# Padding rows by plain transfers, 71 blocks, four output buffers and a last norm in two groups, in a two-layer attention and expert kernel

## The reference

```python
def _layernorm(x, axis=-1, eps=1e-05):
    m = jnp.mean(x, axis=axis, keepdims=True)
    v = jnp.var(x, axis=axis, keepdims=True)
    return (x - m) / jnp.sqrt(v + eps)
...
        E_FFN = 8
        E_ZERO = 4
        TOP_K = 2
        logits = jnp.einsum('btd,ed->bte', x, gate_w) + expert_bias
        topk_logits, topk_idx = jax.lax.top_k(logits, TOP_K)
        topk_w = jax.nn.softmax(topk_logits, axis=-1)
        onehot = jax.nn.one_hot(topk_idx, E_TOT, dtype=x.dtype)
        w = jnp.einsum('btk,btke->bte', topk_w, onehot)
        w_ffn = w[..., :E_FFN]
        w_zero = jnp.sum(w[..., E_FFN:], axis=-1)
        h = jax.nn.silu(jnp.einsum('btd,efd->btef', x, w1))
        y = jnp.einsum('btef,edf->bted', h, w2)
        out = jnp.einsum('bte,bted->btd', w_ffn, y) + w_zero[..., None] * x
        return out
...
    x = _layernorm(x + _L1_ffn_ref(x, L1_ffn_gate_w, L1_ffn_expert_bias, L1_ffn_w1, L1_ffn_w2), axis=-1)
```

## Time and profile before

| | us |
|---|---|
| runs: median | 1774.31 |
| runs: lowest to highest, of 3 | 1770.64 to 1775.97 |
| profiled execution | 1760.04 |
| its span on the core | 1758.3 |
| TensorE busy in the span | 1458.9 (83%) |
| VectorE, ScalarE, GpSimd busy | 930.9, 696.8, 498.6 |

### The profile page before, as it was taken

The page is one execution under the profiler, slowest core; times in us unless marked ns, Lnnn a source line. Parts: engine busy times, 40 slices in busy tenths (PEclk is TensorE's granted clock), DMA queues, the critical chain, the costliest instruction groups (busy, mean ns, idle before and its releaser), DMA issues.

```text
span 1758.3 us, 31304 instructions
## 1 busy us (share of the span) xinstructions
PE 1458.9 (83%) x10329; PEld 957.5 (54%) x10330; DVE 930.9 (53%) x3473; ACT 696.8 (40%) x959; POOL 498.6 (28%) x419
## 2 busy tenths in 40 slices
PE   3688898888889739999469999999998719999990
PEld 1245454454455416666334556555555419999990
DVE  2667768777787411111256656765753343444334
ACT  1144443544544501111036666766676402222223
POOL 4032234234233311212111123132222233444441
PEclk7788888888997859999779999999999859999995
DMA  6744335255252122533153536434526323444445
GB/s 159 196 106 96 84 95 130 80 124 113 71 97 82 50 67 72 130 87 85 36 111 82 116 78 138 111 84 107 125 64 181 136 70 63 70 71 72 72 60 200
DMA packets 118701, 174.52 MB, mean 99 GB/s; under 512 B 17159, under 2 KB 100513, under 8 KB 112432
## 3 DMA queue, kind: packets, MB, share of 16 engines
q1 hardware_dynamic: 95376, 147.65, 34.1%
q0 software_dynamic: 20928, 23.56, 8.6%
q10 hardware_dynamic: 2272, 1.70, 0.4%
HBM read 107.32 MB, written 72.82 MB: 102 GB/s over the span
## 4 chain that ended last, share of the span: by engine, by line
PE 64%; DVE 13%; issue 6%; DMA 4%; ACT 3%; POOL 2%; SPq 0%; DVEq 0%; POOLq 0%; ACTq 0%
PE ST L705 9%; PE OT L723 9%; PE ST L1797 7%; PE shared L1809 6%; PE ST L1263 6%; DVE scratch L1097 4%; PE shared L1452 3%; PE shared L749 3%; PE OT L1271 3%; PE shared L1271 3%; PE shared L766 2%; PE shared L797 2%; PE shared L814 2%; PE shared L1458 1%; PE shared L741 1%
## 5 line engine op out<-in xcount | busy, mean ns | idle before, releaser
L838 ACT ACTIVATE arena<-ST 128x1024 f32<-128x1024 f32 x416 | 414.6, 1024 | 264.0 <-PE ST L705 262.4
L1097 DVE CUSTOM_DVE_ANT_0 scratch<-shared,mask 128x512 bf16<-128x512 f32 (+3 forms) x512 | 228.8, 486 | 86.9 <-PE shared L814 71.8
L705 PE MATMUL ST<-arena 96*128 96x256 bf16 (+2 forms) x1792 | 253.1, 278 | 14.6 <-DMA arena<-qk_parts 13.7
L723 PE MATMUL OT<-arena,v_aug 128*32 128x256 f32 (+1 forms) x3584 | 252.9, 384 | 3.9 <-POOL arena L1165 1.7
L705 PEld LDWEIGHTS ST<-arena 96*128 96x128 bf16 (+1 forms) x1792 | 159.1, 102 | 114.2 <-issue 51.7
L814 PE MATMUL shared<-arena 96*128 96x512 bf16 (+3 forms) x512 | 126.7, 325 | 52.9 <-DVE mx L1097 21.7
L1910 POOL DMA_INDIRECT sum<-arena,block_to_row x72 | 113.5, 1577 | 171.2 <-DMA sum<-arena,block_to_row 128.1
L723 PEld LDWEIGHTS OT<-arena,v_aug 128*32 128x32 f32 x3584 | 85.4, 111 | 117.9 <-issue 69.9
L1165 POOL TENSOR_SCALAR_AFFINE_SELECT arena<-arena 128x512 f32<-128x512 f32 (+1 forms) x96 | 78.7, 820 | 238.4 <-ACT arena L838 238.4
L1809 PE MATMUL shared<-arena 128*128 x576 | 136.5, 380 | 0.0
L814 PEld LDWEIGHTS shared<-arena 96*128 96x128 bf16 x512 | 43.1, 103 | 132.7 <-issue 63.3
(11 more groups left out here) (208 smaller groups left out, 2338.9 us busy)
## 6 DMA issues: line engine op xcount, KB each, us to landing
arena<-qk_parts SPq DMA_DIRECT2D x224, 128.0 KB, 7.1
qk_parts<-qk_src SPq DMA_DIRECT2D x64, 384.0 KB, 2.6
arena<-qk_parts SPq DMA_DIRECT2D x32, 384.0 KB, 4.5
block_rows<-slot_x SPq DMA_DIRECT2D x72, 130.0 KB, 2.4
arena<-qk_parts SPq DMA_DIRECT2D x32, 256.0 KB, 5.3
sum<-x_out SPq DMA_DIRECT2D x16, 512.0 KB, 2.9
arena<-in_experts_inter SPq DMA_DIRECT2D x7, 1024.0 KB, 5.2
arena<-in_experts_out SPq DMA_DIRECT2D x7, 1024.0 KB, 9.5
```

The lines of the kernel that those rows point to most:

```text
L705: mm = pe.matmul(ST[n % 2][:, i * 256 + at:i * 256 + at + nq], K[par][0:rows, h, kb * P:(kb + 1) * P], Q[par][0:rows, h, q0:q0 + nq], star ...
L723: mm = pe.matmul(OT[32 * i:32 * i + 32, q0:q0 + nq], v_aug[par][:, kb, g * GH + i, :], PT[n % RING][:, i, at:at + nq], start=(u == 0), sto ...
L838: act.activation(PT[n % RING][:, :, :], ST[n % 2][:, :].rearrange("p (h n) -> p h n", h=GH), func, scale=ATT_SCALE).then_inc(L["exp"], 1)
L1097: taken = dve.tensor_tensor_reduce(out=junk[n % 2][:, at:at + m], in0=bank[:, at:at + m], in1=mask[:, 0:m], scale=1.0, scalar=LOW, op0=ALU ...
```

## The change

Four edits in one.

1. `pad_rows`: the padding rows are written by plain transfers at a row number read from `t_pad`, for four experts on SP in place of step `("sv", 2)` and for four on ScalarE ahead of the scaling of step `("xs", 2)`. Both wait for `D_PADS`. The eight scatters of `d_pool` are gone. SP's save of the last batch moves behind its first four block loads, and two waits for the saves leave SP's list.
2. `NBLK` is 71. 8192 rows at most, in eight segments, can't start more than 71 blocks of 128 (64, and 7 for the rests). The loops have `LAPS` = 17, the rest is written out.
3. `by` has four buffers, and ScalarE waits for the add of block j − 4. The wait for block j − 2 is now GpSimd's, ahead of its add.
4. The norm has two groups, of five chunks and three, instead of 3 + 3 + 2. Statistics and root are no longer mixed. Of the first five chunks GpSimd writes one row of four (`e_pool`) and ScalarE three; of the last three VectorE writes two and ScalarE two (before: ScalarE all four of six chunks, VectorE three of the last two).

```diff
-NBLK = 2 * NTOK // P + E1
+NBLK = 2 * NTOK // P + E1 - 1
+LAPS = NBLK // 4
...
+        def pad_rows(eng, experts):
+
+            eng.wait_ge(d_chain, D_PADS)
+            settle(eng)
+            for e in experts:
+                row = eng.value_load(t_pad[0:1, e:e + 1], min_val=0, max_val=ZROW)
+                eng.dma_start(slot_x1[bass.ds(row, P), :], no_row[:, :]).then_inc(d_pad, 16)
...
                     elif step == "sv":
+                        if turn.kind == "ninth" and n == 2:
+                            pad_rows(sp, range(0, E1 // 2))
+                            continue
                         save_rows(sp, L, turn, n, sum1)
             slots(sp, emit)
-            for i in range(2):
-                sp.wait_ge(L["x_saved"][i], NB // 2 * 16)
...
                     elif step == "xs":
+                        if turn.kind == "ninth" and n == 2:
+                            pad_rows(act, range(E1 // 2, E1))
                         keep_rows(act, L, turn, n, ROUTE1)
...
-        by = [carve(D) for _ in range(2)]
+        by = [carve(D) for _ in range(RX)]
...
             for j in range(RX):
                 load(j, j)
+            save_rows(sp, LC, Turn("ninth", NB + 1), 2, sum1)
...
-                if not isinstance(j, int) or j >= 2:
-                    act.wait_ge(d_added[(i + 2) % RX], lap * 16 + (16 if i >= 2 else 0))
-                act.activation(by[par], Y_BANK[par][:, 0:D], ACT.Identity, scale=b_gain[:, i:i + 1]
+                wait(act, d_added[i], lap * 16)
+                act.activation(by[i], Y_BANK[par][:, 0:D], ACT.Identity, scale=b_gain[:, i:i + 1]
...
         def d_pool(pool):
-            pool.wait_ge(d_chain, D_PADS)
-            pool.wait_ge(s_zero, 1)
-            for e in range(E1):
-                pool.indirect_dma_start(out=slot_x1,
-                                        out_offset=bass.IndirectOffsetOnAxis(ap=t_pad[:, e:e + 1], axis=0),
...
             def emit(j, i, lap):
 
+                if not isinstance(j, int) or j >= 2:
+                    pool.wait_ge(d_added[(i + 2) % RX], lap * 16 + (16 if i >= 2 else 0))
...
-        E_GROUPS = [(0, 3), (3, 6), (6, N_E)]
-        BY_DVE = {c: (3 if c >= 6 else 0) for c in range(N_E)}
+        E_GROUPS = [(0, 5), (5, N_E)]
+        BY_DVE = {c: (2 if c >= 5 else 0) for c in range(N_E)}
+        BY_POOL = {c: (1 if c < 5 else 0) for c in range(N_E)}
...
+        def e_pool(pool):
+            for g, (c0, c1) in enumerate(E_GROUPS):
+                pool.wait_ge(e_root, g + 1)
+                for c in range(c0, c1):
+                    for t in range((c + 1) * EB - BY_POOL[c], (c + 1) * EB):
+                        pool.tensor_scalar(out=e_all[:, t, :], in0=e_all[:, t, :], scalar1=e_mv[:, t, 0:1],
+                                           scalar2=e_small[:, 2, t:t + 1], op0=ALU.subtract, op1=ALU.mult
+                                           ).then_inc(e_by_pool, 1)
...
-                more = stats(*E_GROUPS[g + 1]) if g + 1 < len(E_GROUPS) else iter(())
-                together(root(c0, c1), more, 1)
+                all_of(root(c0, c1))
+                if g + 1 < len(E_GROUPS):
+                    all_of(stats(*E_GROUPS[g + 1]))
```

More of the change, by code:

```diff
@@ L1750, in d_sp, with refill @@
                 load(j, j)
-            with sp.Fori(0, NBLK // RX - 1) as it:
-                for i in range(RX):
[L1754 to L1761, removed]
+            save_rows(sp, LC, Turn("ninth", NB + 1), 2, sum1)
+            def refill(j, i):
+                sp.wait_ge(d_t, j + 1)
+                settle(sp)
+                sp.wait_ge(d_told, j * 2 + 2)
+                settle(sp)
+                load(j + RX, i)
+            with sp.Fori(0, LAPS - 1) as it:
+                for i in range(RX):
+                    refill(it * RX + i, i)
+            for j in range((LAPS - 1) * RX, NBLK - RX):
+                refill(j, j % RX)
         T_BANK = shared[0]
@@ L1826, in four @@
                     down(j, par, j - 1)
-            passes(pe, NBLK // RX - 1, four)
-            for j in range(NBLK - 3, NBLK):
+            passes(pe, LAPS - 1, four)
+            for j in range((LAPS - 1) * RX + 1, NBLK):
                 if j + 1 < NBLK:
@@ L1839, in blocks @@
                 emit(j, j, 0)
-            with eng.Fori(1, NBLK // RX - 1) as it:
+            with eng.Fori(1, LAPS) as it:
                 for i in range(RX):
                     emit(it * RX + i, i, it)
-            for j in range(NBLK - RX, NBLK):
+            for j in range(LAPS * RX, NBLK):
                 emit(j, j % RX, j // RX)
@@ L1911, in emit @@
                     out=sum1, out_offset=bass.IndirectOffsetOnAxis(ap=b_to_row[:, i:i + 1], axis=0),
-                    in_=by[i % 2], in_offset=None, bounds_check=NTOK + S - 1, compute_op=ALU.add
+                    in_=by[i], in_offset=None, bounds_check=NTOK + S - 1, compute_op=ALU.add
                     ).then_inc(d_added[i], 16)
@@ L1924, in build @@
         e_load = [sem(f"e_load{i}") for i in range(N_E)]
-        e_chain, e_root, e_by_dve, e_by_act, e_out = (
-            sem(x) for x in ("e_norm_chain", "e_root_ready", "e_rows_by_dve", "e_rows_by_act", "e_out"))
-        E_GROUPS = [(0, 3), (3, 6), (6, N_E)]
-        BY_DVE = {c: (3 if c >= 6 else 0) for c in range(N_E)}
+        e_chain, e_root, e_by_dve, e_by_act, e_by_pool, e_out = (
+            sem(x) for x in ("e_norm_chain", "e_root_ready", "e_rows_by_dve", "e_rows_by_act", "e_rows_by_pool", "e_out"))
+        E_GROUPS = [(0, 5), (5, N_E)]
+        BY_DVE = {c: (2 if c >= 5 else 0) for c in range(N_E)}
+        BY_POOL = {c: (1 if c < 5 else 0) for c in range(N_E)}
         def of_rows(ap, i):
@@ L1934, in rows_of @@
             at = c * EB + BY_DVE[c]
-            return range(c * EB, at) if by_dve else range(at, (c + 1) * EB)
+            return range(c * EB, at) if by_dve else range(at, (c + 1) * EB - BY_POOL[c])
         def e_sp(sp):
@@ L1950, in e_sp @@
                 settle(sp)
+                by_pool += BY_POOL[c]
+                wait(sp, e_by_pool, by_pool)
+                settle(sp)
                 sp.dma_start(of_rows(out, c), e_rows[c]).then_inc(e_out, 16)
             sp.wait_ge(e_out, N_E * 16)
+        def e_pool(pool):
[6 more added lines that the diff above has]
+                                           ).then_inc(e_by_pool, 1)
         def e_act(act):
@@ L2048, in _ @@
             d_pool(pool)
+            e_pool(pool)
 def shape_constants():
```

4 lines of the change are left out of this document (1 added, 3 removed).

## The result

The changed kernel takes 1758.54 us (median of 4 runs, 1752.37 to 1759.35), the kernel before 1774.56 in the same comparison (4 runs). The ratio is 0.9904, with a 95% interval of 0.9876 to 0.9931: 16.0 us gained by the medians, 17.0 by the ratio, 12 to 22 by the interval. Forecast were 18.1 us and 1756.

The account below looks back on a forecast made before the run. TensorE was taken to bound the block loop, a chain of waits the handover, load waits then VectorE and ScalarE the last norm. 10.5 + 3.7 + 0 + 3.9 = 18.1 us off the 1774.31 median gives 1756, range 1749 to 1765.

Parts of the forecast that it names:

- Padding rows: Handover into the expert blocks: with eight scatters off GpSimd's queue, it moves from 1438.61 to 1428.1, 10.5 us gained.
- (c): Handover: the padding writes stretch the token scatters to 6.4 us, total 1760; chance 0.10.
- (d): Handover gains nothing, as the save or a padding row lands as late as now: 1766.6 us; chance 0.06.
- The clock: Start of the blocks: same slow start at half clock expected, 0; one block more or fewer at half clock is ±1.8 us.
- One block fewer: Block loop: one pitch of the up product less, 3.7 us gained; 0 taken for the written-out tail.
- Four buffers: Block loop: ScalarE is freed but TensorE's loss, from VectorE's wait, stays; 0 gained, between 0 and 1.7 us.
- rival (a): Head of the block loop loses its 1.7 us after all, because adds come earlier: 1754.5 us; chance 0.08.
- Rival (e): Block loop: with the new wait the adds become the bound, slower, 34 us at a landing of 8.5: 1790; chance 0.03.
- GpSimd's row: Last norm: a row on GpSimd takes 0.6 us, bounds 0.34 to 2.6, hidden below ScalarE's 1.5 us for three rows.
- Rival (b): Last norm: GpSimd's rows over 1.5 us hold the writes; at 2.6 the norm loses 1.3 us: 1761; chance 0.11.
- Its second form: Last norm: by the port rule VectorE's root waits five GpSimd rows of 0.6, taking 3.0 us from the sum: 1759.
- Last norm: End of the kernel: ScalarE ends 3.0 us earlier and the last writes queue less, together 3.9 us gained.

Follow-up runs that it names:

- pads_alone: Kernel before with the padding edit alone: plain transfers on SP and ScalarE, last save behind the first four loads; 1747.94 us, ratio 0.9939.
- own_rows: Changed kernel with row numbers and gains of the first twelve blocks in columns of their own, those blocks written out; 1741.03 us, ratio 0.9895 to the kernel before.
- four_buffers: Kernel before with four buffers of block outputs and the moved wait alone; 1759.6 us, ratio 1.0005.
- two_rows: Changed kernel with GpSimd writing two of four rows of the norm's first five chunks, ScalarE two; 1763.03 us, ratio 0.9938 to the kernel before.
- no_pool_share: Changed kernel with no norm rows on GpSimd, ScalarE doing all four of the first five chunks; 1743.86 us, ratio 0.9922 to the kernel before.
- warm: Changed kernel with twelve more 128x512 products on TensorE between the counts and the first block; 1741.35 us, ratio 0.9908 to the kernel before.
- warm15: Changed kernel with fifteen more products on TensorE between the counts and the first block; 1755.8 us, ratio 0.9887 to the kernel before.

## Why the prediction was right or wrong

The time and the sign were right: the forecast 18.1 us lies inside both intervals (12 to 22 and 11 to 24.5 us), 1.4 to 2.1 us above the gains of the medians and 0.4 to 1.1 above those of the ratios. Term by term, from the traces:

- **Padding rows, 10.5.** Right in mechanism and size: 26.5 to 26.9 us from the counts to the first turn became 15.9 to 16.1, 10.7 on average. As named, the landing of the token scatters is late next, so rivals (c) and (d) fall. Landing of the plain transfers was bounded at 2.1 to 6.4 and taken near 2.1; it is 2.2 to 3.2 in pads_alone.
- **The clock, 0 ± 1.8.** Before, first turn to third up product is 12.02, 9.74, 9.25, 9.74 and 9.74; with the padding edit 9.81, 9.79, 11.47, 11.78, 11.88, 11.67. Two groups of values, 2 us apart, in both kernels. The prediction's ±1.8 for a block more or less at half clock is that difference. That the mean is 1.0 us higher with the edit can be chance; these profiles show neither a loss nor that there is none. What the prediction left out is that the slow start can be had back: 7.55 with TensorE kept busy.
- **One block fewer, 3.7.** Right: 3.73 in the traces, 3.5 by the ratio.
- **Four buffers, 0.** Right, and for the reason given. own_rows takes the named wait away and TensorE's loss with it; rival (a) is refuted by four_buffers. Rival (e), the adds as the bound, is refuted by 223.00 of 223.00 us busy on TensorE.
- **GpSimd's row, 0.6.** The term that was mis-sized: it was scaled by elements from the two-tensor addition, but takes 1.21. No row of before had one tensor and two scalars a partition, and the far end kept in the text, 2.6, was as near by ratio. That the miss cost nothing is in part luck: the row stays under the 1.5 us of ScalarE's three rows, with a margin of 0.3 us where 0.9 was reckoned. Rival (b) put its point of decision there; two_rows crosses it, with 2.4 us a chunk against 1.0, and loses 4.6 to 4.7 us. Its second form, the root held by the port, was priced at 3.0 us: the second root takes 2.56 us in the changed kernel and 2.43 in no_pool_share, 0.13 more.
- **Last norm, 3.9.** First load to end is 33.9 us on average in the five profiles with the old norm (33.3 to 34.4) and 29.7 in the seven with the new one as it is (29.2 to 29.9), some 4.3 less. Behind ScalarE's first row it is 3.3 us where the sum has 3.3 to 3.4; the earlier start was put at 0.6 and is 1.0 on average. As the time to that first row moves by 1 us by itself with either norm, an excess of 0.4 can't be told from the landing of the loads.
- **The sum.** From the traces it is 19.5 without the clock's column, 1.4 above the forecast, while the runs lie 0.4 to 2.1 below it; where the difference goes stays open. The prediction carried the 14.3 us between the profiled execution and the median along as a constant of the kernel. It is not: the kernel before takes 1759.2 and 1758.6 us on two chips and 1774.5 on a third, so this profile is most likely of another chip than the runs. That the absolute time came out at 1758.5 for 1756 is thus owed to the subtraction from the median of the same comparison.

## What to carry to other kernels

Here eight transfers stood behind eight others on one queue, though all sixteen only had to be finished at the same time. Moved to two queues that stood idle, they no longer counted, and the gain was the distance between the two landings, 10.5 us forecast and 10.7 found. Of two waits for the same adds in one loop, removing ScalarE's, 10.6 us long, gave nothing; the one that mattered was found from the row in which the bounding engine waits, followed one step back to the buffer that it guards. Compare profiles from a common instruction just ahead of the edit, and several of each, since the code before it may differ by more than the edit gives.

## What the runs showed of the hardware

- The code up to the counts took 1415 to 1420 us in eight profiles on two chips and 1423 to 1435 in four on a third, and the kernel before took 1759.2, 1758.6, 1774.6 and 1774.5 us in four comparisons. The changed kernel's ratio was 0.9904 in one and 0.99 in another.
- TensorE's granted clock, after the start of the blocks, rose from half to full 4 to 6 us after the first turn in some executions and 9 to 10 us after it in others, in the same code. In warm it was still full at 1431 and at half from 1432 on, after TensorE had stood idle since 1429.3; in warm15 it was full on both sides of an idle of 0.32 us.
- A GpSimd row of 256 float32 elements with two scalars a partition takes 1.21 us, ScalarE's same row 0.50 and VectorE's 0.34. Next to GpSimd's rows, two of the twelve small steps of VectorE's root in two_rows take twice their 0.17 us, and the root's first step takes 0.30 us in the changed kernel and in two_rows, 0.17 in no_pool_share.
